# Experts of an MoE layer: 128-token blocks as the stationary operand of gate and up, activation transposed on TensorE, rests laid out in 71 blocks

## What is computed

```python
logits = x @ router_weight.T                 # x: 4096 x 512, 8 experts
probs = softmax(logits)
top_v, top_i = top_k(probs, 2)               # two experts per token, weights renormalised
for e in range(8):                           # computed for the picked tokens only
    gu = x @ gate_up_proj[e].T               # 704 columns: 352 gate, 352 up
    cur = silu(gu[:, :352]) * gu[:, 352:] @ down_proj[e].T
    out = out + cur * combine[:, e:e+1]
out = out + sigmoid(x @ shared_gate_w.T) * shared   # shared expert, width 1408
```

## Time and profile before

| | us |
|---|---|
| median of 3 runs | 2080.58 |
| lowest and highest | 2074.74, 2081.69 |
| profiled execution, first to last instruction (span) | 2077.8 |
| attention (span's start to 735) | 735 |
| routing (735 to 884) | 149 |
| experts (886.5 to 1411) | 524.5 |
| shared expert (1411 to the end) | 667 |

### The profile page before, as it was taken

How to read it: one execution, slowest core, us unless ns; L and a number is a source line. 1 busy time by engine, 2 the same in 40 slices (tenths; PEclk the granted TensorE clock), 3 DMA queues, 4 the chain that set the end, 5 groups by cost and what they waited for, 6 DMA issues and landing times.

```text
span 2077.8 us, 34931 instructions
## 1 busy us (share of the span) xinstructions
PE 1956.2 (94%) x11932; PEld 1556.9 (75%) x11932; DVE 1160.8 (56%) x2487; ACT 783.0 (38%) x1584; POOL 514.5 (25%) x1106
## 2 busy tenths in 40 slices
PE   4999999999999849999999999998999999999997
PEld 3666666666666427899999999997788878888885
DVE  3566666666665439766776666774532423333234
ACT  2445545555454322355555554553111111111101
POOL 1224334244342333411111111200222112030303
PEclk9799999999999869999999997999999999999999
DMA  5234363453633223366676665775231112031203
GB/s 162 75 113 137 118 190 120 135 151 118 196 117 111 102 70 119 108 213 234 234 247 239 231 235 194 254 242 179 79 122 61 61 62 93 29 122 51 70 20 101
DMA packets 128579, 286.53 MB, mean 138 GB/s; under 512 B 12192, under 2 KB 40864, under 8 KB 119616
## 3 DMA queue, kind: packets, MB, share of 16 engines
q1 hardware_dynamic: 117408, 248.63, 35.3%
q0 software_dynamic: 11040, 36.18, 5.9%
HBM read 205.35 MB, written 76.02 MB: 135 GB/s over the span
## 4 chain that ended last, share of the span: by engine, by line
PE 54%; DMA 1%; DVE 1%; ACT 0%; issue 0%; SPq 0%; POOL 0%; ACTq 0%; POOLq 0%; DVEq 0%
PE sh_bank L1046 19%; PE ex_bank L1046 16%; PE sh_bank L1058 10%; PE ex_bank L1058 8%; PE ex_bank L1631 2%; DMA sh_yk<-shd_in 1%; SPq L1193 0%; DVE sh_up L1946 0%; SPq L1192 0%; ACT sh_up L1894 0%; DVE sh_dn L1946 0%; DMA ys<-sh_yk 0%; ACT sh_dn L1894 0%; DVE sh_gate L1946 0%; DVE sh_stats L129 0%
## 5 line engine op out<-in xcount | busy, mean ns | idle before, releaser
L1046 PE MATMUL ex_bank<-ex_xT,ex_gu 128*128 128x256 f32 (+12 forms) x2808 | 357.6, 284 | 1.0 <-DVE ex_xT L1640 1.0
L1046 PEld LDWEIGHTS ex_bank<-ex_xT,ex_gu 128*128 128x128 f32 (+1 forms) x2808 | 343.8, 185 | 4.9 <-issue 1.2
L1078 DVE TENSOR_TENSOR sh_silu<-sh_silu,sh_bank 128x512 f32<-128x512 f32 x77 | 52.9, 687 | 374.7 <-ACT sh_silu L1071 348.3
L690 DVE TENSOR_REDUCE at_nmax<-at_bank 128x1 fp32r<-128x384 f32 (+3 forms) x512 | 222.2, 476 | 37.4 <-PE at_bank L450 32.1
L1046 PE MATMUL sh_bank<-sh_xT,sh_gate 128*128 128x512 f32 x924 | 229.1, 397 | 8.1 <-DVE sh_gate L1946 3.1
L1071 ACT ACTIVATE sh_silu<-sh_bank 128x512 f32<-128x512 f32 x77 | 45.9, 596 | 497.3 <-PE sh_bank L1046 464.7
L886 ACT ACTIVATE at_PT<-at_bank 128x512 f32<-128x512 f32 (+1 forms) x384 | 184.1, 506 | 123.3 <-PE at_bank L463 95.1
L1058 PE MATMUL sh_bank<-sh_dn,sh_act 128*128 128x512 f32 x924 | 223.4, 391 | 2.2 <-DVE sh_act L1087 2.2
L1046 PE MATMUL sh_bank<-sh_xT,sh_up 128*128 128x512 f32 x924 | 225.0, 392 | 0.0
L1046 PEld LDWEIGHTS sh_bank<-sh_xT,sh_gate 128*128 128x128 f32 x924 | 176.0, 191 | 48.2 <-issue 6.3
L1058 PEld LDWEIGHTS sh_bank<-sh_dn,sh_act 128*128 128x128 f32 x924 | 172.7, 188 | 42.3 <-DVE sh_act L1087 5.9
(11 more groups left out here) (241 smaller groups left out, 2930.5 us busy)
## 6 DMA issues: line engine op xcount, KB each, us to landing
ex_gu_in<-gu_in SPq DMA_DIRECT2D x39, 1408.0 KB
at_Qs<-q_dram SPq DMA_DIRECT2D x96, 256.0 KB, 4.1
ex_dn_in<-dn_in SPq DMA_DIRECT2D x39, 512.0 KB
ys<-sh_yk SPq DMA_DIRECT2D x35, 512.0 KB, 3.1
sh_yk<-x_in SPq DMA_DIRECT2D x16, 1024.0 KB, 5.4
q_dram<-at_q_h SPq DMA_DIRECT2D x64, 256.0 KB, 4.2
xnT<-sh_xT SPq DMA_DIRECT2D x14, 1024.0 KB, 5.7
sh_xT<-xnT SPq DMA_DIRECT2D x14, 1024.0 KB, 7.8
```

Of the source, the lines that this page charges most:

```text
L690: last = nc.vector.tensor_reduce(nmax[:, s % 2, i:i + 1], S_ps[u][:, col:col + (i + 1) * P], AX_X, ALU.max, negate=True)
L1046: last = self.nc.tensor.matmul(self.gate_up_ps[c % 2][which][0:m, 0:w], cols(i, k), self.xT[j][:, k, 0:w], start=(step == 0), stop=(step = ...
L1078: nc.vector.tensor_tensor(silu[c % 2][0:m, 0:w], silu[c % 2][0:m, 0:w], gate_up_ps[c % 2][1][0:m, 0:w], ALU.mult).then_inc(s["product"], 1)
```

## The change

**Layout.** The 7 rest tiles become 7 single blocks of 128 tokens. A rest of more than 128 tokens takes a pair place while there are free ones, and otherwise two singles. Routing finds a rest's place and second place with other VectorE steps. There are still 39 tiles: 32 pairs of blocks and 7 singles, 71 blocks.

**Gate and up.** A block's 128 transposed tokens are stationary and the 352 weight columns move, so gate and up come out with the tokens on the partitions. The product silu(gate) times up (`product`) is then transposed on TensorE, three transposes a block, and split for `down`.

**Order.** The work goes by block. TensorE: gate of block b, transposes of the activation of b-1, transposes of the tokens of b+1, up of b, down of b-1. The weight splitting is no longer spread: ScalarE does `high_gate_up` of the next tile at the end of a tile's last block, VectorE does `low_gate_up` right behind that block's `product`, and the three pieces of the down weights (`high_down`, `low_down`) are split at the head of their own tile. TensorE waits for all four low pieces of gate and up ahead of a tile's first gate. Loads of gate/up and of down have semaphores of their own, and stores go by block, behind the loads of that turn, for the tile before.

The diff, cut to what the text speaks of:

```diff
-FULL = 2 * NB * S // TE
...
-NT = len(PLACE_WIDTH)
-SC = PLACE_COLUMN[NT]
+PAIRS = 2 * NB * S // TE
+SINGLES = E - 1
+NT = PAIRS + SINGLES
+SC = QE * PAIRS + SINGLES
+HOT = SC + SC % 2
...
+for j in range(SINGLES):
+    PLACE_OF += [LOOPED + j, PAIRS + j]
...
+BLOCKS = [QE if p < PAIRS else 1 for p in PLACE_OF]
...
+    def high_gate_up(self, loads, r):
+        self.nc.scalar.wait_ge(self.gu_loaded[r], 16 * loads)
+        for k in range(C):
+            self.nc.scalar.activation(self.gu_s[r][0][:, k, :], self.gu_in[r][:, k, :], ACT.Copy).then_inc(self.hi, 1)
+
+    def low_gate_up(self, n, r):
+        for k in range(C):
+            self.nc.vector.wait_ge(self.hi, self.WN * n + k + 1)
+            self.nc.vector.tensor_tensor(self.gu_s[r][1][:, k, :], self.gu_in[r][:, k, :],
+                                         self.gu_s[r][0][:, k, :].bitcast(F32), ALU.subtract).then_inc(self.lo, 1)
...
+            steps.then_wait(nc.vector.tensor_scalar(in_pair[:], rest_place[:], float(PAIRS), float(2 * NT), ALU.is_lt, ALU.mult))
+            steps.then_wait(nc.vector.tensor_tensor(second_place[:], rest_place[:], in_pair[:], ALU.add))
+            steps.then_wait(nc.vector.tensor_scalar(second_place[:], second_place[:], end[:, E - 1:E], float(E - PAIRS),
+                                                    ALU.add, ALU.add))
...
+            steps.then_wait(nc.vector.tensor_tensor(over[1][:], of_tile, of_expert(second_place[:]), ALU.is_equal))
+            steps.then_wait(nc.vector.tensor_tensor(over[0][:], over[0][:], over[1][:], ALU.add))
...
-            steps.then_wait(nc.vector.tensor_tensor(at_place[:], rest_place[:].unsqueeze(2).to_broadcast([P, E, NT]),
-                                                    place_no[:].unsqueeze(1).to_broadcast([P, E, NT]), ALU.is_equal))
-            steps.then_wait(nc.vector.tensor_tensor(at_place[:], at_place[:],
-                                                    place_base[:].unsqueeze(1).to_broadcast([P, E, NT]), ALU.mult))
-            steps.then_wait(nc.vector.tensor_reduce(shift_rest[:], at_place[:], AX_X, ALU.add))
...
+            def store(b, slot):
+                sp.wait_ge(out_taken, b + 1)
+                column = COLUMN_OF_BLOCK[b] if isinstance(b, int) else b
+                sp.dma_start(ys[:, bass.ds(column, 1), :], y_out[:, slot:slot + 1, :]).then_inc(stored[slot], 16)
...
+                if not known or n + 2 < NT:
+                    e = weights.expert(sp, n + 2)
+                    sp.wait_ge(weights.lo, WN * n + C)
+                    weights.load_gate_up(sp, e, r)
                     sp.wait_ge(weights.lo, WN * n + WN)
-                    weights.load(sp, n + 2, r)
+                    weights.load_down(sp, e, r)
...
-                store(n)
+                if not known:
+                    for i in range(QE):
+                        store(at_tile(n) - QE + i, i)
+                elif n > 0:
+                    for b in range(at_tile(n - 1), at_tile(n)):
+                        store(b, b % SLOTS)
...
+            def gate_or_up(out, which, r, parity):
+                step = 0
+                for k in range(C):
+                    for i, j in PASSES:
+                        last = nc.tensor.matmul(out[:, 0:I_MOE], xT[parity][i][:, k, :],
+                                                weights.gu_s[r][j][:, k, which * I_MOE:(which + 1) * I_MOE],
+                                                start=(step == 0), stop=(step == 3 * C - 1))
+                        step += 1
+                last.then_inc(gate_up_done, 1)
...
+            def transpose_act(b, parity):
+                pe.wait_ge(product_ready, b + 1)
+                for c, m in enumerate(rows):
+                    last = nc.tensor.transpose(act_ps[0:m, c * P:(c + 1) * P], product[parity][:, c * P:c * P + m], idf[:])
+                last.then_inc(act_done, 1)
+
+            def down(n, b, r, parity, first_of_tile):
+                if first_of_tile:
+                    pe.wait_ge(weights.lo, WN * n + WN)
+                if not isinstance(b, int) or b >= 2:
+                    pe.wait_ge(out_taken, b - 1)
...
+            def turn(n, r, pair):
+                known = isinstance(n, int)
+                for i in range(blocks(n)):
+                    b = at_tile(n) + i
...
+                    pe.wait_ge(xT_lo, b + 1)
+                    if i == 0:
+                        pe.wait_ge(weights.lo, WN * n + C)
+                    gate_or_up(gate_ps[parity], 0, r, parity)
+                    if before:
+                        transpose_act(b - 1, 1 - parity)
+                    if not last_block(b):
+                        if i + 1 < blocks(n):
+                            transpose_x(r, i + 1, b + 1)
...
+                    gate_or_up(up_ps[parity], 1, r, parity)
+                    if before:
+                        down(pn, b - 1, pr, 1 - parity, pfirst)
...
             def turn(n, r, pair):
...
                 for i in range(blocks(n)):
-                    act.wait_ge(s["out_done"], blocks_before(n) + i + 1)
...
+                    b = at_tile(n) + i
...
+                    if not known:
+                        take_out(b - 2, i, 2 * pair + r - 1)
+                    elif b >= 2:
+                        take_out(b - 2, (b - 2) % SLOTS, (b - 2) // SLOTS)
+                    if i == 0:
+                        weights.high_down(pair + 1, r)
+                    act.wait_ge(gate_up_done, 2 * b + 1)
+                    nc.scalar.activation(product[parity][:], gate_ps[parity][:, 0:I_MOE], ACT.Silu).then_inc(silu_ready, 1)
+                    if not known or b > 0:
+                        high_act(b - 1, 1 - parity)
+                    if not last_block(b):
+                        high_x(b + 1, 1 - parity)
+                    if i == blocks(n) - 1 and not last_block(b):
+                        act.wait_ge(gate_up_done, 2 * at_tile(n))
+                        weights.high_gate_up(pair + 1 + r, 1 - r)
...
             def turn(n, r, pair):
...
+                for i in range(blocks(n)):
+                    b = at_tile(n) + i
...
+                    if i == 0:
+                        weights.low_down(n, r)
+                    if not known or b > 0:
+                        low_act(b - 1, 1 - parity)
+                    if not last_block(b):
+                        low_x(b + 1, 1 - parity)
+                    dve.wait_ge(silu_ready, b + 1)
+                    dve.wait_ge(gate_up_done, 2 * b + 2)
+                    nc.vector.tensor_tensor(product[parity][:], product[parity][:], up_ps[parity][:, 0:I_MOE],
+                                            ALU.mult).then_inc(product_ready, 1)
+                    if i == blocks(n) - 1 and not last_block(b):
+                        weights.low_gate_up(n + 1, 1 - r)
```

More of the change, by code:

```diff
@@ L1135, in gather, with expert @@
                                     ).then_inc(self.gathered[r], 16)
[L1137 to L1142 removed]
+    def expert(self, sp, n):
+        return sp.value_load(self.tile_expert[0:1, bass.ds(n, 1)], min_val=0, max_val=E - 1)
@@ L1145, in load @@
         sp.dma_start(dn_in[0:last, self.NC - 1, :], self.dn[bass.ds(e, 1), full:I_MOE].rearrange(
-            "o p d -> (o p) d")).then_inc(self.loaded[r], 16)
[L1148 to L1152, removed]
-    def split_hi(self, loads, r, q):
-        self.nc.scalar.wait_ge(self.loaded[r], 48 * loads)
-        self.nc.scalar.activation(self.piece(q, r, 0), self.piece(q, r), ACT.Copy).then_inc(self.hi, 1)
@@ L1643, in turns, with at_tile @@
+        act_done, act_hi, act_lo = sem("act_done"), sem("act_hi"), sem("act_lo")
+        out_done, out_taken = sem("out_done"), sem("out_taken")
+        block = ctx.enter_context(nc.Block())
+        def at_tile(n):
+            return blocks_before(n)
         def turns(engine, turn):
-            with engine.Fori(0, LOOPED // 2) as pair:
+            for n in range(2):
+                turn(n, n % 2, n // 2)
+            with engine.Fori(1, LOOPED // 2) as pair:
                 turn(2 * pair, 0, pair)
@@ new lines, in transpose_act @@
+            def transpose_act(b, parity):
[8 more added lines that the diff above has]
+                    pe.wait_ge(out_taken, b - 1)
+                pe.wait_ge(act_hi, b + 1)
+                out = out_ps[parity]
+                for c, m in enumerate(rows):
+                    nc.tensor.matmul(out[:], act_s[parity][0][0:m, c, :], weights.dn_s[r][0][0:m, c, :],
+                                     start=(c == 0), stop=False)
+                    nc.tensor.matmul(out[:], act_s[parity][0][0:m, c, :], weights.dn_s[r][1][0:m, c, :],
+                                     start=False, stop=False)
+                pe.wait_ge(act_lo, b + 1)
+                for c, m in enumerate(rows):
+                    last = nc.tensor.matmul(out[:], act_s[parity][1][0:m, c, :], weights.dn_s[r][0][0:m, c, :],
+                                            start=False, stop=(c == NC - 1))
```

(3 more changed lines are left out.)

306 lines of the change are left out of this document (148 added, 158 removed).

## The result

| | before | after |
|---|---|---|
| median, us | 2080.15 (4 runs) | 2165.08 (4 runs) |
| lowest and highest | 2074.74, 2081.69 | 2163.05, 2168.22 |
| profiled execution's span | 2077.8 | 2161.3 |

The changed kernel takes 1.0406 times as long, 95% interval 1.0391 to 1.0421: 85 us more, where the prediction had 25 more, in a range that reached to 88 more. The sign and the wait are as forecast. The size is that of the first rival, in which the clock falls at the stalls.

A forecast was written before the change was run, and what follows sets the result against it. TensorE's own work was taken to bound the experts. Stalls outweighing its savings gave +24 there, the experts' head -1, routing +2: +25 on the profiled 2077.8, or about 2106 us, range 2088 to 2168.

The forecast's parts named there:

- the first rival: Experts: the clock halves after tile-end stalls, 1.6 us each; 2167 if all 38, 2136 if half; chance 0.32, shared with DMA delays.
- The added wait: At each of 38 tile ends TensorE waits for gate/up low pieces: path 4.1 us, cover 2.09, stall 2.0, about 1.75 shown.
- TensorE's work: Experts: TensorE needs 13.26 us a pair, 6.63 a single; 474 for 524.6 if it stayed the bound, a gain of 51.
- the rival's 2031: Whole kernel if weight splits come early enough and TensorE stays the limit in the experts: 2031 us, chance 0.08.
- The clock: Experts: whether short tile-end stalls drop TensorE to half clock; the forecast counted no drops, otherwise 1.6 us each.
- the turning point: Tile ends in the experts: the shown stall length, about 1.8 us, that decides whether half clock follows.
- a fall keeps step with the tiles: Experts: a pair with half clock lasts 15.3 + 1.6 and repeats the same stall, so few or most tiles have it.
- the two waits of the earlier trace: Kernel before: 1.84 us in routing, followed by half clock (4.60 for 12 matmuls); 1.80 in the shared expert, not (3.04).
- Head and routing: Start of the experts about 1 us shorter; routing 2 us longer, between 0 and +5, as VectorE steps run into GpSimd's.
- TensorE stays the bound: Experts: splits early enough, no tile-end waits, pairs 13.3 us apart, the gain of 51 stands; 2031 us, chance 0.08.
- The stall was not shorter: Judges a rival: overlapping instructions make each tile-end stall 1.4 us instead of 2.0, 23 less, 2083, no change; chance 0.08.
- singles did bring their gain: Judges a rival: singles gain nothing, their period set by weights; 2144 if DMA is late too; chance 0.32 shared with clock falls.

The follow-up runs named there:

- one filling matmul: Changed kernel with one 512-column matmul, its result overwritten, put ahead of the wait at each tile's end: 2118.28 us, ratio 1.0187 to the kernel before.
- both edits: Changed kernel with next tile's gate/up pieces split after a tile's first block, and first gate using high weights first, awaiting low pieces singly: 2036.96 us, ratio 0.9804.
- seven inserted matmuls: Changed kernel with seven extra 512-column matmuls in the middle of each tile's first block, the wait at the tile's end kept: 2179.87 us, ratio 1.0482.
- with four: Changed kernel with four extra 512-column matmuls in the middle of each tile's first block, the wait at the tile's end kept: 2168.14 us, ratio 1.0423.
- filling work: Changed kernel with 7, 2 or 1 matmuls of 512 columns, results overwritten, ahead of each tile-end wait: 2111.47, 2110.09 and 2118.28 us.

## Where the prediction failed, and what of it was right

**The added wait: right.** 4.1 of path against 2.09 of cover gave a stall of 2.0, of which 1.75 shown. Shown are 1.72 to 1.90, 68.3 in all for 38 x 1.75 = 66.5, and what the waits cost is 2110.1 - 2037.0 = 73, 1.9 a tile. Pairs without a fall take 15.4 for 15.3, singles 8.8 (1296.97 to 1305.78, with one filling matmul, above) for 8.65. No wait is named for DMA or GpSimd at the tiles; for ScalarE there is one of 0.8, at the last block.

**TensorE's work: a term mis-sized by 10 us.** I read 0.160 for a matmul of 352 columns off a straight line. 12 take 2.0 (1053.22 to 1055.24, transposes behind them), 0.166 to 0.168; by 1704 matmuls that is 10 us and more. With both edits and no waits the stage takes 483.5, not 474, and the kernel 2037, not the rival's 2031.

**The clock: the step that failed.** The prediction saw that a short stall can be followed by half clock, and then put that cost at nothing: it set the turning point at 1.8, just above its own stall of 1.75. The forecast thus had no falls, with a chance of 0.52, and the rival had them at 1.6 each: 2167 if all fell. 33 of 38 did, at 1.66, behind waits of 1.72 to 1.90. Of the 59 us that the forecast lacks, 55 are this. The stage came out at 609.4 for the 549 of the sum, 60 more: 55 of falls and some 10 of work, less about 5 that is not traced; routing is 2 more than put down, and what follows the experts 4 less. That the time lies inside the range is due to the range's upper end, which is the rival's.

I had written that a fall keeps step with the tiles, so that few or most would fall. That held for the changed kernel (33 of 38) and with seven inserted matmuls (3), not with four (16, in turn). The turning point of 1.8 didn't hold: 1.72 had falls, and 1.90 had none at times. So the 0.04 between the two waits of the earlier trace rows need not be what told them apart. With two rows of about that length, one of each kind, nothing favoured "holds" over "falls", and the forecast should have had them level, with both prices named.

The Trainium skill, "TensorE: Matmul & The Clock Gate", section "Why this matters for your kernels", warns only of idle gaps between bursts of matmuls that are longer than these. The 33 falls behind waits of 1.72 to 1.90 show that shorter ones are not safe. The skill's section "HAM oscillation — how this bites in real kernels" describes a clock that falls again at every repeat of a loop, there behind longer waits. The changed kernel does that behind these.

**Head and routing: near.** The head is 1.1 shorter for 1, and the first gate comes without half clock. That was luck: with seven matmuls inserted further down, the same head, with the same wait of 1.41 ahead of the first gate, had it (3.58 for 2.17). Routing was put at +2, for one blocking of VectorE by GpSimd; the transposes of the experts are 4.0 later, of which 1.1 were there ahead of the changed steps (the first matmuls of line 1364 begin at 773.56, their likes at 772.42 before). VectorE and GpSimd in the changed kernel, as the earlier trace rows:

```profile
803.05 0.48 DVE L1560 TENSOR_TENSOR ro_over<-ro_tile_place,ro_second_place 128x312 f32<-128x312 f32 x1
...
803.27 2.52 POOL L1325 TENSOR_TENSOR ro_gu<-sh_yk,ro_gu 128x1024 fp32r<-128x1024 f32 x1 [6.45 <-ACT ro_gu L1430]
803.57 2.57 DVE L1561 TENSOR_TENSOR ro_over<-ro_over 128x312 f32<-128x312 f32 x1
...
805.76 1.50 POOL L1330 TENSOR_TENSOR ro_dn<-sh_yk,ro_dn 128x512 fp32r<-128x512 f32 x1
806.17 1.42 DVE L1562 TENSOR_TENSOR ro_over<-ro_over,ro_expert_no 128x312 f32<-128x312 f32 x1
```

Two steps in a row end within 0.4 of GpSimd's instructions, and take 2.57 and 1.42 for the 0.48 of like steps: the shift that the prediction worked out, with a second blocking. TensorE's wait behind it is 4.00 for 1.84, as the earlier trace rows:

```profile
810.15 5.49 PE L1390 MATMUL ro_bank<-ro_dn,sh_xT 128*128 128x512 f32 x12 [4.00 <-DVE sh_xT L1474]
```

**The rivals.** "TensorE stays the bound" is what both edits together reach: its mechanism was sound, its condition was not met. The stall was not shorter, and singles did bring their gain: with both edits one takes 6.7 (1223.93 to 1230.62), for 6.63 in the sum. No wait of TensorE in the experts is named for DMA.

## What to carry to other kernels

When a change gathers work that an engine used to spread over a tile, walk the path from the last operand to the first use and set it against what covers it; here that gave the wait to within 0.2 us. Then price a short wait that recurs in every tile twice, as idle time and as half clock behind it, and if the trace has waits of that length of both kinds, treat both prices as equally likely. Look for half clock in the kernel before as well, also where its engine never waits. Reordering a sum so that the late operand is used last took the wait away, and with it the falls, at no cost in work.

## What the runs showed of the hardware that I had not expected

- Waits of TensorE at a tile's end: 1.26 to 1.59 in the runs with filling work, no fall; 1.65 to 1.67, a fall behind 4 of 15; 1.72 to 1.90, behind 33, 16 or 3 of 38, with waits that are the same in all three and other matmuls inserted between them.
- A fall doesn't begin at one point. In the changed kernel the granted clock went to 0.50 some 1.4 us after TensorE was back at work at 1084.06 (2.84 for 2.17 there, and 0.84 for the 0.49 of the transposes behind), and some 0.1 after it at 1389.15 (3.72). From fall to fall of that series the first gate mostly takes longer, until one, at 1426.96, has no fall.
- The clock also falls without a wait: in the kernel before, in the rest tiles of 32 and 64 columns, it stood at 0.50 from 1245 to 1255 and from 1274 to 1284 with TensorE busy for all of that time.
- More work can cost nothing where it takes away falls: 7 matmuls of 512 columns a tile ahead of the wait made the kernel 54 us faster.
